# Moving the gate projection to the ring of two projection banks, and reordering a slot of a Mamba-2 layer on TensorE, ScalarE and VectorE

## What is computed

```python
proj = einsum('bsd,de->bse', rmsnorm(layernorm(x)), in_proj_w)     # z, xBC, dt
xBC  = silu(causal_conv4(xBC) + conv_b)                            # 4 taps a channel
xs, Bg, Cg = split(xBC)                                            # 32 heads of 64; 8 groups of 64
dt = softplus(dt_raw + dt_bias);  dA = exp(-dt * exp(A_log))
h  = dA_t * h + (dt_t * x_t) B_t^T;   y_t = h C_t                  # the scan over tokens
g  = (y + D * xs) * silu(z)                                        # z is the gate
g  = g * rsqrt(mean_group(g^2) + eps) * gate_norm_w                # groups of 256 channels
x  = x + g @ out_proj_w
x  = x + ffn(layernorm(x))
```

## Time and profile before

| | us |
|---|---|
| median of 3 runs | 1456.59 (1456.51 to 1459.61) |
| the profiled execution | 1454.48 |
| its span in the trace | 1452.8 |
| busy in the span: PE / DVE / POOL / ACT | 1174.6 / 1094.2 / 893.9 / 778.0 |

### The profile page before, as it was taken

One profiled execution on the slowest core, in us unless ns is written; L12 is line 12 of the kernel. 1 busy time (PEld: TensorE's weight loads), 2 busy tenths in 40 slices (PEclk: granted clock), 3 DMA queues, 4 the chain that ended last, 5 costly groups with the idle time before them and its releaser, 6 DMA issues.

```text
span 1452.8 us, 43522 instructions
## 1 busy us (share of the span) xinstructions
PE 1174.6 (81%) x15222; PEld 789.1 (54%) x15222; DVE 1094.2 (75%) x2357; ACT 778.0 (54%) x2058; POOL 893.9 (62%) x848
## 2 busy tenths in 40 slices
PE   2346889898888889887989798979898998886787
PEld 2324565565555555555656555655565565553456
DVE  8735988787678768776878577868787888745895
ACT  2535666555565546554656455656565656531443
POOL 2612577676576657775767576757776777675222
PEclk9975999899899989998999899979999999897999
DMA  5331222222222212222222122222221222111211
GB/s 134 145 88 50 50 71 77 56 60 61 57 71 60 60 54 77 58 65 61 77 60 60 54 74 60 60 69 66 58 70 52 73 64 65 56 34 31 95 32 34
DMA packets 88881, 94.40 MB, mean 65 GB/s; under 512 B 22736, under 2 KB 66384, under 8 KB 88400
## 3 DMA queue, kind: packets, MB, share of 16 engines
q1 hardware_dynamic: 84432, 89.37, 22.0%
q10 hardware_dynamic: 4224, 2.10, 0.5%
HBM read 81.99 MB, written 9.44 MB: 63 GB/s over the span
## 4 chain that ended last, share of the span: by engine, by line
PE 62%; issue 11%; DVE 10%; ACT 8%; POOL 6%; DMA 1%; SPq 1%; ACTq 1%; DVEq 1%; POOLq 0%
PE bank L1339 10%; PE bank L1327 7%; PE bank L1350 7%; PE bank L1454 7%; PE bank L1286 6%; PE bank L1290 6%; PE bank L1443 6%; PE bank L1287 4%; ACT gate L856 2%; ACT xdt L832 2%; PE bank L1408 2%; POOL gated L635 2%; DVE hpk L1068 1%; POOL gated L620 1%; POOL cdec L630 1%
## 5 line engine op out<-in xcount | busy, mean ns | idle before, releaser
L1054 DVE SCALAR_TENSOR_TENSOR conv<-bank,cw,conv 128x511 f32<-128x511 f32 (+2 forms) x576 | 428.0, 743 | 41.5 <-ACT conv L765 39.8
L620 POOL TENSOR_TENSOR gated<-gated,gate 128x512 f32<-128x512 f32 x128 | 163.1, 1274 | 157.4 <-DVE gated L1016 157.4
L641 POOL TENSOR_TENSOR ssum<-ssum,sq 128x512 f32<-128x512 f32 x96 | 123.6, 1288 | 205.6 <-ACT sq L851 205.6
L832 ACT ACTIVATE xdt<-bank,dt_all 128x64 f32<-128x64 f32 x1024 | 223.8, 339 | 20.1 <-DVE xw L1043 20.1
L1068 DVE SCALAR_TENSOR_TENSOR hpk<-hpk,pend,bank 128x64 f32<-128x64 f32 x768 | 211.9, 276 | 12.9 <-DVE hpk L1068 1.0
L1339 PE MATMUL bank<-gated,w_out 128*128 128x512 f32 x256 | 170.5, 754 | 59.1 <-ACT cbs L794 15.7
L856 ACT ACTIVATE gate<-bank 128x512 f32<-128x512 f32 x128 | 76.6, 598 | 241.6 <-PE bank L1290 241.6
L613 POOL TENSOR_TENSOR lm<-lm,cbs 128x512 f32<-128x512 f32 x128 | 163.3, 1275 | 53.9 <-ACT cbs L794 38.2
L765 ACT ACTIVATE conv<-bank,cb_bias,cw 128x512 f32<-128x512 f32 x192 | 149.0, 776 | 69.5 <-PE bank L1290 51.0
L1350 PE MATMUL bank<-ident_t,chan 128*128 128x128 f32 x512 | 128.9, 323 | 65.2 <-ACT gate L856 42.8
L1286 PE MATMUL bank<-xn_hi,w_hi 128*128 (+1 forms) x320 | 162.0, 506 | 23.5 <-ACT xdt L832 23.5
(11 more groups left out here) (175 smaller groups left out, 1749.2 us busy)
## 6 DMA issues: line engine op xcount, KB each, us to landing
spread<-decay_scratch SPq DMA_DIRECT2D x256, 128.0 KB, 3.3
spread<-product_scratch SPq DMA_DIRECT2D x256, 128.0 KB, 3.8
lm<-in_L_attn_in_proj_w SPq DMA_DIRECT2D x1, 2048.0 KB, 8.7
xn_scratch<-chan SPq DMA_DIRECT2D x4, 512.0 KB, 5.1
r_stage<-residual_scratch SPq DMA_DIRECT2D x8, 256.0 KB, 2.7
x_scratch<-r_stage SPq DMA_DIRECT2D x8, 256.0 KB, 3.1
cbs<-x_scratch SPq DMA_DIRECT2D x8, 256.0 KB, 2.8
gated<-x_scratch SPq DMA_DIRECT2D x1, 2048.0 KB, 9.0
```

What stands on the lines that cost most here:

```text
L620: gp.tensor_tensor(gated[:, v % 2, mr, :], gated[:, v % 2, mr, :], gate[:, mr, :], ALU.mult).then_inc(gated_done, 1)
L832: act.activation(xdt[:, r, at:at + HP], xt_bank[:, at:at + HP], ACT.Copy, scale=dt_h).then_inc(xdt_done, 1)
L1054: V.scalar_tensor_tensor(out=conv[:, ci % 4, shift:S], in0=tile_bank(b, n, t)[:, 0:S - shift], scalar=cw[:, q, t, KW - 1 - shift:KW - shif ...
```

## The change

The gate projection leaves bank 5 and takes its place in the ring of banks 0 and 1 with the other tiles, ten in a unit (`PROJ`); `proj_free` makes each projection wait for the reader of the bank's last content: the last tap of a tile, or the gate's silu. The x transposes now wait for the previous slot's xdt instead of its gate, and the gate projection no longer waits for xdt. The slot's first tile is projected in its own slot, between the two halves of the states, and not at the end of the slot before. The variance moves behind the intra matmuls, into the ring bank that the gate projection will use; ScalarE copies it instead of VectorE, ahead of xdt. The gate projection runs before the inter matmuls in r = 3 and after them in the other slots. On ScalarE the silu of the first tile comes ahead of `start_tile`, and sq ahead of xdt. `ORDER` is new.

```diff
-ORDER = {0: "0123456", 1: "01T23T456T", 2: "0T1T2T3T4T56T"}
+ORDER = {0: "0123456", 1: "0T123T456T", 2: "0T1T23T45T6TT"}
...
-assert NCONV % 2 == 0
+PROJ = [(4 * q + r, t) for q in range(UNITS) for r in range(R) for t in PLAN[r] + ["z"]]
+assert len(PROJ) % 2 == 0
...
-            if isinstance(b, int) and b == 0 and n < R:
+            if isinstance(b, int) and b == 0 and n < R and t != "z":
                 return bank[FIRST_BANKS[CONV_ORDER.index((0, t))]]
-            return proj_bank[CONV_ORDER.index((n // R, t)) % 2]
+            return proj_bank[PROJ.index((n, t)) % 2]
...
+                finish_tile(0)
                 if real:
                     start_tile(PLAN[r][0])
-                if prev is not None:
-                    bb, m = prev
-                    pq, prr = divmod(m, R)
-                    for t in PLAN[prr]:
-                        i = CONV_ORDER.index((pq, t))
-                        after(act, tap, NTAP, bb, TAP[pq, t, KW - 1])
-
-                        if t == 0:
-                            after(act, bt_ready, UNITS, bb, pq - 1)
-                            after(act, cb_ready, UNITS, bb, pq - 1)
-                        elif t == 1:
-                            after(act, cdec_done, SLOTS, bb, 4 * (pq - 2) + 3)
-                        else:
-                            skip_there(act, bb, 4 * (pq - 2) + t - 2)
-                        act.activation(chan[:, chan_of(pq, t), :], conv[:, i % 4, :], ACT.Silu).then_inc(silu_done, 1)
+                finish_tile(1)
...
+                if r == 0 and back(b, n, LAG_VAR) is not None:
+
+                    bb, m = back(b, n, LAG_VAR)
+                    v = m // R
+                    after(act, var_ready, UNITS, bb, v)
+                    after(act, rstd_done, UNITS, bb, v - 1)
+                    act.activation(vtok[:, :], tile_bank(b, n, "z")[:, 0:2 * CH], ACT.Identity, scale=1.0 / (DI // G),
+                                   bias=eps_c[:, 0:1]).then_inc(var_copied, 1)
...
-                    act.activation(gate[:, m % R, :], xt_bank[:, :], ACT.Silu).then_inc(gate_done, 1)
+                    act.activation(gate[:, m % R, :], tile_bank(b, n, "z")[:, :], ACT.Silu).then_inc(gate_done, 1)
...
+            def proj_free(b, i):
+
+                bb = b
+                while True:
+                    i -= 2
+                    if i < 0:
+                        i, bb = i + len(PROJ), bb - 1
+                        if isinstance(bb, int) and bb < 0:
+                            return
+                    pn, pt = PROJ[i]
+                    who = back(bb, pn, LAG_SSD if pt == "z" else 0)
+                    if who is not None:
+                        break
+                if pt == "z":
+                    after(pe, gate_done, SLOTS, *who)
+                else:
+                    after(pe, tap, NTAP, bb, TAP[pn // R, pt, KW - 1])
...
+                def gate_projection():
+
+                    bb, m = ssd
+                    if r == 0 and back(b, n, LAG_VAR) is not None:
+                        vb, vm = back(b, n, LAG_VAR)
+                        after(pe, var_copied, UNITS, vb, vm // R)
+                    else:
+                        proj_free(b, PROJ.index((n, "z")))
+                    three_passes(tile_bank(b, n, "z")[:, :], (m // R, CONVS + m % R), bb, z_ready)
...
-                    after(pe, gate_done, SLOTS, bb, m - 1)
+                    xdt_there(pe, bb, m - 1)
...
+                if real:
+                    project(b, n, PLAN[r][0])
...
+                two = real and len(PLAN[r]) == 2
+                var = r == 0 and back(b, n, LAG_VAR) is not None
+                if two:
                     project(b, n, PLAN[r][1], y_inputs)
-                    if yy is not None:
-                        y_intra()
-                    if yy is not None:
-                        intra_finished()
-                    if ssd is not None or st is None:
-                        out_projection()
-                    if yy is not None:
-                        y_inter()
                 else:
                     y_inputs()
-                    if ssd is not None or st is None:
+                    if ssd is not None:
                         out_projection()
-                    if yy is not None:
-                        y_intra()
-                    if real:
-                        project_next()
-                    if yy is not None:
-                        if not real or own_first(*((b, n + 1) if n + 1 < SLOTS else (NB, 0))) or (n + 1 == SLOTS and following(b) is None):
-                            intra_finished()
-                        y_inter()
-                if ssd is not None:
-                    bb, m = ssd
-                    xdt_there(pe, bb, m)
-                    three_passes(xt_bank[:, :], (m // R, CONVS + m % R), bb, z_ready)
-                if real and len(PLAN[r]) == 2:
-                    project_next()
+                if yy is not None:
+                    y_intra()
+                    intra_finished()
+                if two and ssd is not None:
+                    out_projection()
+                if var:
+                    variance()
+                if ssd is not None and not two and not var:
+                    gate_projection()
+                if yy is not None:
+                    y_inter()
+                if ssd is not None and (two or var):
+                    gate_projection()
```

## The result

| | before | after |
|---|---|---|
| median, us | 1456.55 (1452.94 to 1459.61, 4 runs) | 1381.12 (1368.21 to 1384.83, 4 runs) |
| the profiled execution | 1454.48 | 1383.45 |
| its span | 1452.8 | 1381.7 |
| mean granted clock | 0.908 | 0.923 |

The ratio is 0.9467, interval 0.94 to 0.9534: the change takes 75 us off, where 41 were forecast.

What follows compares the result with a forecast made beforehand. TensorE, busy 1174.6 of 1452.8 us, was taken as the bound. Terms of -19 us at full clock and -22 us of clock took the profiled 1454.5 to 1413, plus 2.1 to the median: 1415 us, range 1393 to 1458.

Steps and rivals of the forecast that it cites:

- rival 1: Falls of the clock stay or move, leaving only the full-clock sum and the loop's +4: 1442 us, chance 0.18.
- rival 2: The removed wait becomes another ahead of xdt, 0.22 us in each of 64 double slots: 1456 us, chance 0.10.
- rival 3: ScalarE's sq, ahead of xdt, waits for GpSimd's gated tile, 0.6 us 96 times: slower, 1473 us, chance 0.15.
- Rival 4: All works, the clock falls no more in slots 4 to 14, small terms 9 us less: 1395 us, chance 0.10.
- The sum at full clock: TensorE's path without clock effects: -42.8 - 13 + 16 + 13 + 8 = -19 us.
- I take +0.25, +16 us: Double slots: two projections that stood together now stand alone, +0.14 to +0.26 in 64 slots, +16 us taken.
- the pair of transposes: First tile between the state halves covers the second transposes' wait for the first states: -0.11 in some 120 slots, -13 us.
- The term for intra's bare end: Single slots: intra's end loses its covering projection, +0.2 in 64 slots, +13 us.
- The variance* takes its old time: Moved variance costs TensorE the same; its ScalarE copy delays the next transposes 0.25 us, 31 times, +8 us.
- The clock was forecast at -22: Fewer clock falls: r = 0 -17 with two falls left, slot 7 -6, slot 14 -3, loop's turn +4.
- +0.6 in six turns, +4: At a loop's turn the new batch's first tile is done in slow slot 0, no longer ahead: +4 us.
- thin, 0.4 to 0.6 us: Double slots: VectorE's later work costs nothing, but its cover before TensorE would wait is only 0.4 to 0.6 us.

Runs made afterwards that it cites:

- run 1: The changed kernel with only the old ORDER table of state steps put back; 1372.1 us, ratio 0.9422 to the kernel before.
- run 4: The kernel before with the gate's silu on 128 of 512 columns, part of the computation left out; 1428.85 us, ratio 0.9823.
- Run 5: The changed kernel with the variance back between the state halves, copied by VectorE, and r = 0's gate projection ahead of inter; 1369.36 us, ratio 0.9446.
- run 11: The changed kernel timed once more, unchanged, on another chip; 1384.78 us, ratio 0.9527 to the kernel before.
- run 12: The changed kernel with the first tile projected at the previous slot's end and the variance back among the states; 1446.89 us, ratio 0.9982.
- Run 2: The changed kernel with the slot's first tile projected behind both state halves instead of between them; 1479.81 us, ratio 1.0181 to the kernel before.
- run 9: The changed kernel with the next slot's first tile projected at the end of the slot, in the new ring; 1415.88 us, ratio 0.9753.
- run 7: The kernel before with its loop over batches written out on each engine; 1424.25 us, ratio 0.9817 to the kernel before.
- run 3: The changed kernel with ScalarE's square moved from ahead of xdt to behind it; 1365.0 us, ratio 0.938 to the kernel before.

## Why the prediction was too cautious

**Right in direction and in mechanism.** The wait for the gate went, xdt is what the transposes wait for, 0.22 us and in r = 1 (forecast 0.25, at most 0.3), r = 0 takes 9.03 to 9.12 us (9.0 to 9.3), the 0.37 us ahead of the second tile's last pass stayed, `ORDER` did nothing (run 1), and none of rivals 1, 2 and 3 came. The sign "at most 0.3 us for xdt, only in r = 1" did not hold ahead of slot 15, where TensorE waits 1.64 to 1.75 us; the prediction had placed that wait ("the next transposes want the same xdt"), and it stands for the 2.04 us at which the gate projection of slot 14 waited for xdt in before. Rival 4 was nearest in kind, all works and the clock is kept, but its 1395 was still 14 us too long.

**The sum at full clock was -19; it measured -49** (1.59 us in some 31 units). By kind of slot:

| | forecast | measured |
|---|---|---|
| 64 double slots | -0.11 + 0.25 each, +9 | -0.20 each, -13 |
| 31 slots r = 3 | -0.71 - 0.11 + 0.2, -19 | -0.81 each, -25 |
| 31 slots r = 0 | as r = 3, with +0.25, -11 | -0.34 each, -11 |

(The forecast's column adds up to -21, since it counts 62 waits for the gate and 126 pairs of transposes where the sum had 60 and 120.)

The step that failed is one term of the sum, "I take +0.25, +16 us" for two projections that stood together and now stand alone. They cost 2 x 0.81 = 1.62 us, against 1.66 before: -0.04. The 0.96 us that I took as the price of a projection with transposes behind it held a wait for the gate: 0.39 us behind the last pass instead of 0.25, which the list of waits did not count (run 4). The forecast's 2 x 0.96 thus charged the kernel after, twice, a wait that the change removes. Without it the pair cost 1.52, and separating it costs 0.10 and not 0.25. This term accounts for 19 of the 30 us. So the listed 42.8 us were not the whole of the wait for the gate: each slot had 0.14 us beside it. With that the terms add up to what was measured, in r = 3 -0.71 - 0.14 - 0.16 + 0.2 = -0.81, in a double slot -0.14 + 0.10 - 0.16 = -0.20.

The second term is the pair of transposes, forecast -0.11 and measured -0.16 us, 120 times: 6 us more; both pairs' difference in the earlier trace rows was 0.11, and what else they waited for no row names. The term for intra's bare end held in r = 3.

That r = 0 came out as forecast, -0.34 for -0.37, is luck. It has the same hidden 0.14 and the same 0.16 as r = 3, so it should have gained 0.2 more. Against that stand two things that the prediction had too small. The wait for xdt, read as above from the last pass to the transposes, is 0.62 less 0.25, some 0.37 us and not the listed 0.22 (forecast 0.25). And the variance behind intra meets a pause of 0.26 us where the other slots have 0.16. "*The variance* takes its old time" thus missed some 0.2 us in each r = 0: -0.71 - 0.14 - 0.16 + 0.2 + 0.37 + 0.10 = -0.34. Run 5, which takes the variance back, gains 0.58.

**The clock was forecast at -22.** In r = 0 the step said two falls left; none is left, -19 (ten falls at its own 1.5 us would have been -15, it wrote -17). Slots 7 and 14, forecast -6 and -3, gave -6 and -5. For the loop's turn "+0.6 in six turns, +4" measured +17 in the first trace, of which the longer pauses (4.0 us on average for 3.6) are 2 and 27 us more at half clock some 14. In run 11's trace it is +3, so this miss is in part chance of the execution. The clock's terms thus came to -13. Some 13 us more went where the steps had no term, mostly in the written-out batches 0 and 7 (mean clock of batch 0: 0.839 before, 0.893 after; of batch 7: 0.913 and 0.972). So the 34 us between 1415 and 1381 are 30 too few at full clock, 13 without a term, and 9 too many for the clock.

**The reason given for the clock** was right in its main part, the row of narrow matmuls. Of the "pauses of 0.69 and 0.8 us around them" the first was not needed (run 12 falls without it). The second stands in every slot that fell, and in 11 of the 12 of before the clock falls in it or less than 0.7 us behind it; it isn't enough by itself, and whether it is needed no run shows.

**VectorE's cover,** "thin, 0.4 to 0.6 us", was right and was underused: it was the one number in the prediction that said how much the place of the first tile matters. Run 2 is 100 us slower than after with the tile later, in part through ScalarE's copy, and run 9 is 35 us slower with it earlier, when the bank's last tap is not done.

What stays open: what sets the length of the slow stretch behind a loop's turn, which differs from batch to batch and from run to run (slots 15, 0 and 1 take 33 to 38 us in one trace); how much of the two medians of after and of run 1 is chance in it; and what the pause for cbs adds to the falls in r = 0.

## What to carry to other kernels

Before a group's own time is used as a price, look at what its last row waits for on the weight load as well, and at how far that row stands from the next: here a wait shorter than the modelled end of a matmul was in no list of TensorE's waits, and it turned a gain into a forecast loss. When two engines share a slot nearly evenly, the place at which the first one hands over its first tile can be worth more than the waits that a profile lists, since it starts the other engines' rounds (run 2: 100 us). And a stretch of narrow matmuls like this one wants a wide piece of work in its midst. What a loop's turn costs is best measured by writing the loop out once, and in more than one execution.

## What the runs showed of the hardware

**The granted clock falls around narrow work, with little idle time.** In run 12 TensorE is busy 9.16 of 10.10 us in a slot at PEclk 0.83; the fall comes in a pause of 0.77 us behind 3.4 us of narrow matmuls. In run 4 it comes in three slots while TensorE is busy without a gap. The traces with that row unbroken (before, runs 4, 7 and 12) have 12, 15, 9 and 14 slots of 21 below full clock. The ten with a projection in it or with the variance elsewhere have one slot of 210, in run 3, and that one was slow from slot 7 on.

**A turn of a loop** comes with a pause of TensorE, 2.7 to 4.1 us in before and 3.0 to 4.8 in after, and most often with a stretch at 1.2 GHz; without the loop the kernel before is 27 us faster and after 41 to 50. Behind a single turn the slow stretch was up to 20 us long (batch 4, slots 0 and 1). A turn is not the only thing that brings it: slot 15 of the written-out before runs at PEclk 0.62 with none.

**A small ScalarE copy with a bias from memory.** The answer on the line of the variance's copy (count, min/median/max in ns, first and last start):

```profile
L852 ACT ACTIVATE vtok<-bank,eps_c x32: 267/267/269, 181.3 to 1254.6; 128x8 f32<-128x8 f32 x32
```

It is 0.27 us for eight elements. The Trainium skill, ScalarE: Activation LUTs, section What ACT_TABLE_LOAD costs, gives about 280 ns and 0.833 ns an element for an ACTIVATE whose bias is a pointer, by which the estimate for this one is 0.29 us; the trace agrees within 0.02. The bounds from the rows were 0.22 and 0.69, and 0.2 was taken.
